# First biases of the routed groups: from two TensorE products to a VectorE addition with rows read per group

## The reference, cut to what matters

```
scores = softmax(xt @ gate_w.T)
topk_w, topk_idx = top_k(scores, 3)            # weights divided by their sum
h = einsum('td,efd->etf', xt, fc1_w) + fc1_b[:, None, :]     # 512 columns, per expert
xh, g = h[..., :256], h[..., 256:]
a = gelu(g) * xh * geglu_mult
yexp = einsum('etf,edf->etd', a, fc2_w) + fc2_b
y = einsum('etd,te->td', yexp, comb)           # + the shared expert, then a layer norm
```

## Time and profile before

| | us |
|---|---|
| median of 3 runs | 227.68 (227.41 to 229.1) |
| profiled execution, its own time | 229.41 |
| its span | 227.6 |
| TensorE busy in the span | 214.5 (94%) |
| VectorE, ScalarE, GpSimd busy | 96.0 (42%), 93.6 (41%), 107.4 (47%) |
| routed groups, first input transpose to first product of the last sum | 132.19 to 209.22 |
| mean granted TensorE clock | 0.981 |

### The profile page before, as it was taken

One profiled execution on the slowest core, in us unless ns is written; L12 is line 12 of the kernel. 1 busy time (PEld: TensorE's weight loads), 2 busy tenths in 40 slices (PEclk: granted clock), 3 DMA queues, 4 the chain that ended last, 5 costly groups with the idle time before them and its releaser, 6 DMA issues.

```text
span 227.6 us, 4480 instructions
## 1 busy us (share of the span) xinstructions
PE 214.5 (94%) x1585; PEld 135.7 (60%) x1585; DVE 96.0 (42%) x262; ACT 93.6 (41%) x217; POOL 107.4 (47%) x149
## 2 busy tenths in 40 slices
PE   7999899888997999999999989999999999998992
PEld 4776577676784567766877733454443544434681
DVE  3165561868982320243689845221221212212044
ACT  2003645477674384454221432244433443334123
POOL 0030018487512399999970360555565564434000
PEclk9999999999998599999999999999999999999998
DMA  6999999200002991000110030298646232201552
GB/s 225 401 376 387 360 416 412 120 4 3 3 0 75 420 424 54 0 0 0 49 60 0 23 97 23 53 334 311 221 141 207 79 84 70 70 26 69 174 187 90
DMA packets 11647, 34.41 MB, mean 151 GB/s; under 512 B 2426, under 2 KB 4139, under 8 KB 11628
## 3 DMA queue, kind: packets, MB, share of 16 engines
q1 hardware_dynamic: 9612, 28.65, 33.7%
q0 software_dynamic: 2016, 5.51, 8.1%
HBM read 25.43 MB, written 4.01 MB: 129 GB/s over the span
## 4 chain that ended last, share of the span: by engine, by line
PE 82%; ACT 6%; DMA 5%; issue 3%; DVE 2%; POOL 1%; SPq 0%; ACTq 0%; POOLq 0%; DVEq 0%
PE ps L350 73%; PE ps L1673 3%; PE ps L1480 3%; DMA wres<-y_dram 3%; PE ps L1717 2%; ACT pair_mem L680 2%; ACT pair_mem L686 2%; DMA embed_sb<-embed 2%; DMA y_dram<-ln_mem,dest_i 1%; POOL y_dram L574 1%; ACT L605 1%; PE ps L1590 1%; PE ps L1359 0%; DVE ln_mem L878 0%; SPq L393 0%
## 5 line engine op out<-in xcount | busy, mean ns | idle before, releaser
L350 PE MATMUL ps<-wres,cT 128*64 (+1 forms) x360 | 68.1, 470 | 0.6 <-DVE cT L1266 0.6
L350 PEld LDWEIGHTS ps<-wres,cT 128*64 128x64 f32 (+1 forms) x360 | 24.8, 130 | 24.4 <-issue 16.5
L574 POOL DMA_INDIRECT y_dram<-ln_mem,dest_i x21 | 20.8, 988 | 35.0 <-ACT ln_mem L762 33.9
L1259 DVE TENSOR_TENSOR h<-ps,h 128x256 f32<-128x256 f32 x21 | 8.9, 425 | 54.2 <-ACT h L756 37.9
L565 POOL DMA_INDIRECT embed_sb<-x_dram,gather_i x21 | 20.7, 986 | 16.4 <-DVE gather_i L1191 10.3
L535 POOL TENSOR_SCALAR wres<-wres,mult 128x256 f32<-128x256 f32 x30 | 27.3, 923 | 0.0
L363 POOL TENSOR_TENSOR wres<-wres,cst_sb 128x148 f32<-128x148 f32 x24 | 10.9, 484 | 21.8 <-DVE wres L900 19.4
L756 ACT ACTIVATE h<-ps 128x256 f32<-128x256 f32 x21 | 8.1, 384 | 29.7 <-PE ps L350 25.9
L350 PE MATMUL ps<-h,stage 128*128 128x296 f32 x64 | 17.9, 419 | 0.0
L762 ACT ACTIVATE ln_mem<-ps 128x256 f32<-128x256 f32 x21 | 8.1, 384 | 19.4 <-PE ps L350 16.0
L1673 PEld LDWEIGHTS ps<-cst_sb,embed_sb 128*128 128x128 f32 x42 | 4.3, 141 | 16.4 <-issue 16.2
(11 more groups left out here) (201 smaller groups left out, 385.4 us busy)
## 6 DMA issues: line engine op xcount, KB each, us to landing
wres<-experts SPq DMA_DIRECT2D x15, 768.0 KB, 13.0
embed_sb<-embed SPq DMA_DIRECT2D x6, 416.0 KB, 5.3
wres<-ut SPq DMA_DIRECT2D x3, 768.0 KB, 9.0
stage<-shared SPq DMA_DIRECT2D x2, 771.0 KB, 13.5
wres<-y_dram SPq DMA_DIRECT2D x4, 384.0 KB, 4.9
stage<-wres SPq DMA_DIRECT2D x2, 512.0 KB
f1v<-fc_v SPq DMA_DIRECT2D x1, 512.0 KB
f2u<-fc_u SPq DMA_DIRECT2D x1, 512.0 KB
```

Source lines behind the costliest of these rows:

```text
L350: return nc.tensor.matmul(o, w, x, start=start, stop=stop)
L574: pool.indirect_dma_start(out=y_dram[:, :], out_offset=bass.IndirectOffsetOnAxis(ap=dest_i[:, column(i):column(i) + 1], axis=0), in_=ys[:, ...
L1259: nc.vector.tensor_tensor(a_r[:, i % 2], ps[:, 4 + i % 2, 0:F], gel_r[:, i % 2], ALU.mult).then_inc(a_done, 1)
```

## The change

The biases are no longer products. The DRAM tensor `bias1` becomes 15 x 64 rows of 512, each expert's row 64 times, so that a tile's 64 slots read 64 rows. SyncE reads, for each group, one block of 64 rows for the lower tile and one for the upper into one of three buffers (`biases`, in the memory that `sel` had). VectorE adds them to the PSUM bank into `hid` in SBUF; gate and product read `hid`. The bf16 parts, `sel` and the instructions that make them go. The order on ScalarE becomes `tile_in(i+1)`, `gate(i)`, `tile_out(i-2)`; the weight copies move from SyncE's queue to ScalarE's, half a pair per step in steps 1 to 12; the diagonals start one step later. SyncE's store and read of the routing weights come after the last bias load.

```diff
+NB = 3
             for e in range(NS):
                 sp.dma_start(stage[:, e], shared[:, e]).then_inc(ld_sh[e], 16)
-            sp.dma_start(bias_f[:, :], bias1).then_inc(ld_rte, 16)
...
+            def load_biases(i):
+                at = column(i)
+                e = sp.value_load(owner_i[0:1, at:at + 1], min_val=0, max_val=E - 1)
+                if i >= NB:
+                    sp.wait_ge(hid_done, i - NB + 1)
+                sp.dma_start(biases[0:TM, i % NB], bias1[bass.ds(e * TM, TM), :]) \
+                    .then_inc(ld_b[i % NB], 16)
+                if i < E:
+                    own = bias1[i * TM:(i + 1) * TM, :]
+                else:
+                    e = sp.value_load(owner_i[0:1, NT + i - E:NT + i - E + 1], min_val=0, max_val=E - 1)
+                    own = bias1[bass.ds(e * TM, TM), :]
+                sp.dma_start(biases[TM:P, i % NB], own).then_inc(ld_b[i % NB], 16)
+            def weights_to_rows():
+                sp.wait_ge(comb_done, 2)
...
             sp.wait_ge(own_done, 2)
-            sp.wait_ge(scaled, FC * (NS + E))
-            for k in range(NCOPY):
-                e = sp.value_load(owner_i[0:1, NT + k:NT + k + 1], min_val=0, max_val=E - 1)
-                sp.wait_ge(f1_mm, 2 * k + 1)
-                sp.dma_start(copy_w1[k], wres[:, bass.ds(e * WC, W1C)]).then_inc(ld_copy, 16)
-                sp.dma_start(copy_w2[k], wres[:, bass.ds(e * WC + W1C, W2C)]).then_inc(ld_copy, 16)
+            for i in range(NT):
+                load_biases(i)
+            weights_to_rows()
...
             def gate(i):
-                act.wait_ge(f1_mm, i + 1)
+                act.wait_ge(hid_done, i + 1)
                 if i >= 2:
                     act.wait_ge(a_done, i - 1)
-                nc.scalar.activation(gel_r[:, i % 2], ps[:, 4 + i % 2, F:2 * F], ACT.Gelu).then_inc(ge_done, 1)
+                nc.scalar.activation(gel_r[:, i % 2], hid[:, i % 2, F:2 * F], ACT.Gelu).then_inc(ge_done, 1)
...
+            def copy_expert(k, part):
+                at = NT + k
+                if part == 0:
+                    copied[k] = act.value_load(owner_i[0:1, at:at + 1], min_val=0, max_val=E - 1)
+                    if k == 0:
+                        act.wait_ge(scaled, FC * (NS + E))
+                    act.wait_ge(f1_mm, 2 * k + 1)
+                    nc.scalar.dma_start(copy_w1[k], wres[:, bass.ds(copied[k] * WC, W1C)]).then_inc(ld_copy, 16)
+                else:
+                    nc.scalar.dma_start(copy_w2[k], wres[:, bass.ds(copied[k] * WC + W1C, W2C)]).then_inc(ld_copy, 16)
             for i in range(NT):
-                gate(i)
                 if i + 1 < NT:
                     tile_in(i + 1)
+                gate(i)
                 if i >= 2:
                     tile_out(i - 2)
-                if 4 <= i < 4 + TOPK * TT:
-                    diagonal(i - 4)
+                if 1 <= i <= 2 * NCOPY:
+                    copy_expert((i - 1) // 2, (i - 1) % 2)
+                if 5 <= i < 5 + TOPK * TT:
+                    diagonal(i - 5)
...
+            def add_bias(i):
+                dve.wait_ge(f1_mm, i + 1)
+                dve.wait_ge(ld_b[i % NB], 32 * (i // NB + 1))
+                nc.vector.tensor_tensor(hid[:, i % 2], ps[:, 4 + i % 2, :], biases[:, i % NB], ALU.add) \
+                    .then_inc(hid_done, 1)
...
-                nc.vector.tensor_tensor(a_r[:, i % 2], ps[:, 4 + i % 2, 0:F], gel_r[:, i % 2],
+                nc.vector.tensor_tensor(a_r[:, i % 2], hid[:, i % 2, 0:F], gel_r[:, i % 2],
                                         ALU.mult).then_inc(a_done, 1)
...
             for i in range(NT):
-                gated(i)
+                add_bias(i)
                 if i >= 1:
                     gated_in(i - 1)
+                gated(i)
...
             def first(i):
                 pe.wait_ge(xt_done, i + 1)
                 if i >= 2:
-                    pe.wait_ge(a_done, i - 1)
+                    pe.wait_ge(hid_done, i - 1)
                 if i == 0:
-                    pe.wait_ge(bias_done, 2)
-                    pe.wait_ge(sel_base, 1)
-                    pe.wait_ge(sel_over, 2)
                     pe.wait_ge(scaled, FC * (NS + E))
...
-                for half_rows, level in ((slice(0, TM), 0), (slice(TM, P), 1)):
-                    mm(ps[half_rows, 4 + i % 2, :], sel[0:BIAS_ROWS, column(i), level], bias_t[:, :], True, False)
                 for c in range(DC):
                     for rows, weights in weights_1(i, c):
-                        last = mm(ps[rows, 4 + i % 2, :], xT[:, i % 2, c, rows], weights, False, c == DC - 1)
+                        last = mm(ps[rows, 4 + i % 2, :], xT[:, i % 2, c, rows], weights, c == 0, c == DC - 1)
...
+    arrays["bias1"] = np.repeat(b1[NS:], TM, axis=0)
```

More of the change, by code:

```diff
@@ L109 @@
 C_PLACE, C_FIRST = _col(1), _col(TOPK * TT)
-C_DST, C_DUMP, C_SELROW = _col(TOPK * TT), _col(NT), _col(1)
+C_DST, C_DUMP = _col(TOPK * TT), _col(NT)
 NRTE = _v
@@ L214, in vit_tower_kernel @@
         mult = sb("mult", [P, E * FC])
[L215 to L217 removed]
+        hid = sb("hid", [P, 2, 2 * F])
         rte = sb("rte", [P, NRTE])
@@ L234, in vit_tower_kernel @@
         owner_i = sb("owner_i", [P, NOVER], I32)
-        sel_mem = fac_mem[:, 0:NT * P // 2].bitcast(BF16)
-        sel = sel_mem.rearrange("p (i h s) -> p i h s", i=NT, h=PT)
+        biases = fac_mem[:, 0:NB * 2 * F].rearrange("p (j f) -> p j f", j=NB)
         tab = sb("tab", [P, 2, NT])
@@ L317, in vit_tower_kernel @@
         y_mm, y_done = sem("y_mm"), sem("y_done")
-        scaled, sel_base, sel_over, bias_done, bias_step = (
-            sem(n) for n in ("scaled", "sel_base", "sel_over", "bias_done", "bias_step"))
+        scaled, hid_done = sem("scaled"), sem("hid_done")
+        ld_b = [sem(f"ld_b{j}") for j in range(NB)]
         xr_mm, xr_out = sem("xr_mm"), sem("xr_out")
@@ L448, in _ @@
             sp.dma_start(x_dram[(TT - 1) * P:T, :], rows_st[0:LAST, TT - 1]).then_inc(st_x, 16)
[L450 to L455, removed]
-            sp.wait_ge(own_done, 2)
-            sp.wait_ge(scaled, FC * (NS + E))
-            for k in range(NCOPY):
-                e = sp.value_load(owner_i[0:1, NT + k:NT + k + 1], min_val=0, max_val=E - 1)
-                sp.wait_ge(f1_mm, 2 * k + 1)
-                sp.dma_start(copy_w1[k], wres[:, bass.ds(e * WC, W1C)]).then_inc(ld_copy, 16)
-                sp.dma_start(copy_w2[k], wres[:, bass.ds(e * WC + W1C, W2C)]).then_inc(ld_copy, 16)
+            def load_biases(i):
[13 more added lines that the diff above has]
+                sp.wait_ge(comb_done, 2)
+                for q in range(4):
+                    rows = comb_dram.rearrange("e (t q c) -> e t q c", q=4, c=32)[:, :, q, :]
+                    sp.dma_start(rows, combT[32 * q:32 * q + NE, :, :]).then_inc(st_comb, 16)
+                sp.wait_ge(st_comb, 64)
+                sp.dma_start(comb17[:, :], comb_dram[:, 0:T]).then_inc(ld_c17, 16)
+            sp.wait_ge(own_done, 2)
+            for i in range(NT):
+                load_biases(i)
+            weights_to_rows()
             rows_written(sp)
@@ L1203, in tables @@
                                         ALU.max).then_inc(idx_done, 1)
-            def selectors():
-                dve.wait_ge(sel_base, 1)
-                dve.wait_ge(own_done, 2)
-                for level, at, lo, hi in ((0, 0, 0, NT), (1, 0, NT, NOVER)):
-                    nc.vector.tensor_scalar(sel[:, at:at + hi - lo, level],
-                                            owner_f[:, lo:hi].unsqueeze(2).to_broadcast([P, hi - lo, TM]),
-                                            rte[:, C_SELROW:C_SELROW + 1], None, ALU.is_equal).then_inc(sel_over, 1)
             def routing(k):
@@ L1836 @@
     arrays["mults"] = np.concatenate([columns(mult[e]) for e in range(NS, NE)], axis=1)
-    bias1 = np.zeros((BIAS_ROWS, 2 * F), f32)
-    for q in range(3):
-        bias1[32 * q:32 * q + E] = b1[NS:]
-    arrays["bias1"] = bias1
+    arrays["bias1"] = np.repeat(b1[NS:], TM, axis=0)
     e_, q_ = np.arange(E), np.arange(TOPK * TT)
     token = (q_ % TT)[None, :] * P + p
-    selrow = np.where((p % 32 < E) & (p < BIAS_ROWS), p % 32, -1)
     arrays["rtes"] = np.concatenate([
```

26 lines of the change are left out of this document (6 added, 20 removed).

## The result

The changed kernel took 225.34 us (median of 12 runs, 223.51 to 228.41), the kernel before beside it 228.33 (12 runs, 227.16 to 233.59): ratio 0.9862, interval 0.9817 to 0.9907. By the ratio that is 3.2 us off (by the medians 3.0) where 4.7 were forecast. Two later series timed the same changed kernel again, and they don't agree: 0.9818 (0.9775 to 0.9861), and then, on the same chip, **1.025 (1.0182 to 1.0318)**. A ratio compares only the fast runs of each kernel and leaves out those more than 1.5% above its fastest, which have a lower granted clock, while a median counts all runs.

The account below looks back on a forecast made before the run. TensorE alone was taken to bound the routed stage, 3.54 us a group. Gains of 4.6 (bias pair) and 0.1 (ahead of the stage), 4.7 off the 227.68 median, gave 223.0 us; range 221.8 to 226.5.

Parts of the forecast that it names:

- The bias pair: TensorE, routed stage: removing two bf16 products saves 0.22 us a group, 3.54 to 3.32; 4.6 us over 21 groups.
- 21 x 0.22: TensorE, routed stage: the full 0.22 us is saved in each of 21 groups, first ones included; 4.6 us.
- Ahead of the stage: Before the routed groups: two selector instructions leave VectorE; gain bounded by 0 and 0.3 us, taken as 0.1.
- VectorE: Per group: the added 128x512 addition takes 0.69 us, gated result ready 1.7 after the first products; hidden, cost nothing.
- rule of the shared port pair: VectorE's gate product, now with two SBUF inputs: a GpSimd issue could hold it up to 1.0 us; sum 223.3, taken 0.
- ScalarE's queue: Weight copies moved there: loads 0.86 us, issues 0.5 to 1.10; next input copy still in time, cost taken 0.
- SyncE: Bias reads fit within a group, landings up to 8.0 us hidden; combined weights' later read costs nothing.
- (c): Rival: bias rows land late, holding VectorE's addition and then TensorE; 230.7 us at a 10 us landing; chance 0.09.

Follow-up runs that it names:

- gather_first: Changed kernel with GpSimd issuing the gather for group i+6 ahead of the scatter of group i; 225.31 us, ratio 0.9812 to the kernel before.
- bias_once: Changed kernel reading bias rows for the first three groups only, later groups adding those same rows (wrong biases); 226.91 us, ratio 0.9883.
- no_pair: Kernel before without the two bf16 bias products of each group, nothing else changed (first biases missing); 226.61 us, ratio 0.9886.
- hold_bias: Changed kernel with SyncE's first bias reads held until the first gather has landed; 225.03 us, ratio 0.9835.
- combined: Changed kernel with gathers ahead of scatters, first inputs transposed ahead, and first bias reads held until the first gather landed; 222.83 us, ratio 0.979.
- after_again: Changed kernel, unmodified, timed again with a second profile; 224.67 us, ratio 0.9818 to the kernel before.
- after: Changed kernel in its first timing, with its first profile; 225.34 us, ratio 0.9862 to the kernel before.
- before_act: Kernel before with only ScalarE's new order and the weight copies on its queue, bias products kept; 228.48 us, ratio 0.9998.
- two_buffers: Changed kernel with two bias buffers instead of three, one run; 238.47 us, where the changed kernel took 233.27 in that series.
- after_third: Changed kernel, unmodified, timed again as a control in the third series; 233.27 us, ratio 1.025 to the kernel before.

## Why the prediction was right, and what it missed

**The bias pair: right.** Forecast 3.32 us a group, measured 3.32 in 16 of 17 groups of the loop of the first profile (the other 3.48), and in every one of `gather_first` and `bias_once`. 17 x 0.22 = 3.74 us.

**The first three steps: mis-sized.** I took 0.22 in all 21 groups. The first three distances fell only from 2.92, 2.96 and 2.97 to 2.87 each, 0.24 in sum instead of 0.66. In these steps TensorE waits for ScalarE's copy of the input before its first products. The third of them, before and then after:

```profile
138.98 0.11 PEld L350 LDWEIGHTS ps<-bias_t,fac_mem 96*64 96x64 bf16 x2 [0.49 <-ACT cT L749]
138.98 0.41 PE L350 MATMUL ps<-bias_t,fac_mem 96*64 96x512 bf16 x2 [0.26 <-ACT cT L749]
139.08 0.28 PEld L350 LDWEIGHTS ps<-wres,cT 128*64 128x64 f32 x4
```
```profile
142.16 0.20 PEld L347 LDWEIGHTS ps<-wres,cT 128*64 128x64 f32 x4 [0.58 <-issue]
142.16 1.08 PE L347 MATMUL ps<-wres,cT 128*64 x4 [0.35 <-ACT cT L744]
```

The bias pair stood behind that wait with a short weight load of its own (0.11), and the first float32 weights were loaded under its columns. Without it their load stands bare behind the wait, which grows from 0.26 to 0.35. In the other groups it runs under the products before it. The step that failed is "21 x 0.22": a removed instruction pays in full only where the next one is ready. The end, 8.03 to 7.67, gave 0.36 where 0.22 was counted: 0.21 is the pair (`no_pair` has 7.82), and 0.15 comes from VectorE's new order, since TensorE waits there for the copy of a gated tile, which starts 0.72 after the transposes instead of 0.87. Undisturbed, stage and end together went from 77.03 to 72.69 (`gather_first`), 4.34 against 4.6.

**Ahead of the stage: wrong sign, small.** I took a gain of 0.1. The first transpose follows the start of the gathers' indices by 4.45 and 4.73 us in the changed kernel, by 4.25 before: 0.2 to 0.5 lost, as the first bias reads leave at the same moment as the first gathers. `hold_bias` and `combined` (4.14 both) bear it out; the totals can't tell it apart.

**The gathers: not in my list.** I counted their bytes and never asked how late they may land. In the first profile TensorE's weight loads waited 1.4 us for them, of which all but 0.16 was covered (a register load that began 0.3 ahead of its transposes, at 163.6, made the group 3.48). In `after_again` the stage lost 1.6 us and in `no_pair` 1.9, of which 1.2 and 1.3 fell in the group behind a late gather, whose register load had lost its cover. `no_pair` separates the causes: the shorter group alone can do it.

GpSimd's gathers run six groups ahead by number, but each stands behind a scatter, so in time it is three groups: from a gather's issue to its transposes pass 6.94 us in the loop before and 6.28 after, 3 x 0.22 less. The latest gathers landed 5.9, 6.7 and 6.5 us after their issue (`after`, `after_again`, `no_pair`), all within the old lead and two of them beyond the new one. The Trainium skill, "DMA: Bandwidth & Descriptors", SWDGE vs HWDGE, has GpSimd's DMAs run on the same 16 engines as those of the other queues. The median landings agree: 3.0 and 3.1 us without bias reads and 3.9 to 4.1 with them, at a share of 0.92 in the window above.

By the profiles all these terms leave 4.0 of the 4.7 in the first one and 2.2 in `after_again`, where the two series gave 3.2 and 4.2. They have the right size, but they vary from execution to execution, and no run assigns the rest.

**VectorE: right.** The addition took 0.69 us in all 21 groups, as estimated, with a latency of 1.65 against 1.7. The product with two SBUF inputs kept its 0.43 in all 21 groups. That says less than it seems: in the first profile 14 of them overlap an issue of GpSimd by 0.05 us or less and six by nothing, and only one, at 148.64, runs inside a gather's issue (148.23 to 149.21). It took 0.43 as well, and so did its like in `after_again` (144.90). So the delay that the Trainium skill's rule of the shared port pair would have allowed ("SBUF — State Buffer", Terms) didn't show where it could have, though the earlier trace rows had agreed in kind.

**ScalarE's queue: right.** A load of 0.28 (forecast 0.86, taken from SyncE under traffic) and issues of 0.49 to 0.59; `before_act` is 0.9998. Why the loads fell is not shown; in `before_act`, without bias rows, ScalarE's took 0.28 too, and TensorE's kept their 0.31. **SyncE: right.** Bias rows in 2.7 to 4.5 us against a bound of 8.0, `two_buffers` lists no wait for them, and the read of the combined weights was issued at 202.73, 5.5 us before their use. With the 4.1 us that it took to land in `two_buffers`, 1.4 us of that was slack.

**The size of the whole.** 225.34 lies 2.3 above the forecast of 223.0 and inside the range. Of the 2.3, 0.65 is that the base of the later runs was 228.33 and not 227.68, the rest is the terms above. The third series's 233.27 is outside the range, and none of my cases has it. The one that gave a slower kernel, (c), named a different wait, and what delays the results in that series is open. I can't claim that the change is always a gain. It was one in the first two of three series that timed it; in the third it was a loss. The four kernels of the second series of experiments, on another chip, were all faster than before (0.9754 to 0.9883).

## What to carry to other kernels

Price a removed instruction by the distance between its neighbours, and only in the iterations where the neighbour behind it is ready; then look at every producer that works a fixed number of steps ahead, because its lead in us shrinks with the step. Read that lead off the trace, from issue to use, not off the number in the loop. Compare stages, not spans, where the clock dips elsewhere. And time a variant in several series before calling it better: one kernel had here two tight intervals, 0.9775 to 0.9861 and 1.0182 to 1.0318, on one chip.

## What the runs showed of the hardware

- A gather of 128 rows landed in 2.8 to 5.9 us, median 4.0, with 273 GB/s in a window of the loop (`after`). With the later bias reads left out it was 2.7 to 5.1, median 3.6 (`bias_once`), and with none 2.7 to 4.8, median 3.0 (`before_act`).
- A register load had a median of 0.28 us on ScalarE's and SyncE's queues and grew to 0.46 and 0.67 there, where SyncE's had a median of 0.86 in the copies of before. Behind a wait on TensorE's queue such a load took 0.97 and 1.10 us and left the array idle for 0.98 and 1.11 (`after_again`, `no_pair`).
- A 128x512 addition from PSUM took VectorE 0.69 us, a 128x256 product of two SBUF inputs 0.43, also inside an indirect issue of GpSimd (one case each in `after` and `after_again`).
- Results of TensorE reached two engines 0.7 to 2.6 us late in four groups of `after_third`, at a granted clock of 1.00 in the one shown. The cause is open.
